# Moving query pieces and context splits inside an attention kernel's hand-written order, and issuing its weight and value loads from SyncE

## The chip, the cores and the metric

The kernel runs on one core of a Trainium2 chip, as one launch. The metric is the device time of that launch in microseconds, and the median of several runs is compared. TensorE is called PE in the profile, VectorE DVE, ScalarE ACT, GpSimd POOL and SyncE SP.

## What is computed

One attention block over 16 images of 30 by 30 tokens (900 tokens) with 512 channels and 8 heads of 64, all in f32:

```
q, k, v = x @ wq + bq, x @ wk + bk, x @ wv + bv          # per head, 64 channels
scores  = q @ k.T / sqrt(64) + spatial_bias[|dh| + |dw|]
ctx     = softmax(scores) @ v
resid   = ctx @ wo + bo + x
out     = layernorm(resid) * gamma + beta
```

## The kernel before

**Tiling.** Heads are taken in pairs, four pairs an image (`PAIRS`). A pair has 15 units (`PER_PAIR`), and a unit is two grid rows of queries against all 900 keys, for both heads. So an image has 60 units (`UNITS`). The kernel counts units within an image; unit 60 is unit 0 of the next image.

**The steps of a unit.** PE computes `scores` into one of two PSUM slots (L734). DVE adds the spatial bias and takes the smallest value (`biased_scores`, L1035). ACT takes the exponentials (`exponentials`, L862). POOL joins the halves of each softmax sum (`leads`, `totals`, L1174 to L1191), with one small exponential on ACT in between (`ratios`, L870). ACT multiplies by the weight (`normalise`, L878). DVE transposes (`turn`, L1052). After five units PE multiplies by the values (`context`, L752) and ACT keeps the result (`keep_context`, L893). There are three such groups in a pair and twelve in an image.

**Four engines, one written order.** Each engine runs a `body(im, u)` for every unit in order, and the engines meet only through semaphores. At step u PE issues the scores of units u+6 and u+7 (even u only, `AHEAD` is 6), then contexts due at u (`PV_UNITS`), then the background work of `GAPS[u]`. DVE at step u does `biased_scores(u + 6)` and then `turn(u)`. ACT does what `EVICT` puts at u, the exponentials of u+6 and the normalisation of u+2. Scores of unit n wait until DVE has read unit n-2 from PSUM (`scores_min`).

**Background work.** Everything else that PE does stands in `GAPS`, in one list for all images:

```
("piece", p, j)   # projection for pair p: j = 0, 1 the two key halves, j = 2, 3 the two query halves
("value", t)      # value projection of 128 tokens of the next image
("out", t)        # output projection of 128 tokens of the image before
```

Pieces of pair 4 and pair 5 are those of pairs 0 and 1 of the next image. Each of these jobs is 12 matmuls into one of two PSUM banks, which alternate in the order of the list (`BANK`). A job waits until the bank's last content was evicted. Pieces are evicted by ACT (`keep_piece`, L813), out tiles by DVE (`out_sum` from L1066, `out_norm` L1080), values by ACT (`stage_value`, L835). Pieces use weights in `w_sb`, one buffer for keys and one for queries, which is loaded anew for each pair (`next_weights`, L791). The values of a pair come from DRAM in four loads (`load_values`, L852, at the units of `LOADS`).

**Out tiles.** Before PE can do ("out", t), POOL splits the context tile into a high and a low part (`split_context`, L1202 and L1204, at the units of `SPLIT_UNITS`). It also adds the bias to the residual (`add_bias`, L1240) and makes the reciprocal deviation (`reciprocal_std`, L1246, L1249) that `out_norm` waits for. In the first image there are no out tiles.

**Queues.** SyncE issues all loads of x, the residuals, the stores of the output and of staged values, each behind the waits of its own order (`load_x` L538, `load_residual` L542, `store` L554, `keep_value` L524). ScalarE issues `next_weights` and `load_values` between its computations.

Of the kernel before, what the change touches and what calls it, by code (L numbers as in the profile page):

```python
# [17 lines left out]
NT = FULL + 1  # L18
# [18 lines left out]
KEY, QUERY = 0, 1  # L37
PIECES = [(KEY, 0), (KEY, 1), (QUERY, 0), (QUERY, 1)]
# [8 lines left out]
SPLIT_UNITS = [0, 0, 3, 5, 9, 13, 15]  # L47
# [23 lines left out]
def out(t):  # L71
    return ("out", t)


GAPS = {2: [out(0)] + pieces(1, (3,)), 4: [out(1)], 8: [out(2)] + pieces(2, (0,)), 12: [out(3)] + pieces(2, (1,)),
        14: [out(4)] + pieces(2, (2,)), 18: [out(5)] + pieces(2, (3,)), 22: [out(6)] + pieces(3, (0,)), 24: pieces(3, (2, 1)),
        28: pieces(3, (3,)), 32: [value(0), value(1)], 34: [value(2)], 38: [value(3), value(4)], 42: [value(5), value(6)],
        44: pieces(4, (0,)), 48: pieces(4, (1, 2)), 52: pieces(4, (3,)) + pieces(5, (0,)), 54: pieces(5, (1,)),
        58: pieces(5, (2,))}
# [8 lines left out]
PROLOGUE = [("first_xt", t) for t in range(NT)] + pieces(4) + [value(t) for t in range(NT)] + pieces(5, (0, 1, 2)) + [("bv_wo", 0)]  # L88
PROLOGUE_STEPS = {-6: [value(0), value(1), value(2)], -4: [value(3), value(4), value(5)],
                  -2: [value(6), value(7)] + pieces(5, (0, 1, 2)) + [("bv_wo", 0)]}  # L90
# [173 lines left out]
def attention_layernorm(nc, x, wq, bq, wk, bk, wv, bv, wo, bo, gamma, beta, spatial_bias, out):  # L264
# [3 lines left out]
    with ExitStack() as ctx:  # L268
# [202 lines left out]
        def _(sp):  # L471
# [59 lines left out]

            def load_x(b, t, a):

                n = x_rows(t)
                blocks, m = -(-n // QUAD), min(QUAD, n)
                part = bass.AP(tensor=x.tensor, offset=x.offset + (b * S + XB * t) * D + QUAD * a,
                               ap=[[D, m], [128, KT], [QUAD * D, blocks], [1, QUAD]])
                sp.dma_start(x_nat[QUAD * a:QUAD * a + m, x_slot(t), 0:KT * blocks * QUAD].rearrange(  # L538
                    "p (k b c) -> p k b c", k=KT, b=blocks), part).then_inc(x_in[x_slot(t)], 16)
# [16 lines left out]
            def body(im, u):  # L556
# [5 lines left out]
                if u < 0:  # L562
                    for work in PROLOGUE_STEPS.get(u - 1, []):
                        if work[0] == "value":
                            keep_value(pro, work[1])
                            if work[1] == FULL:
                                rest_values(0)
                    if u == -5:
                        for dst, src in ((bo_all, bo), (gamma_all, gamma), (beta_all, beta)):
                            sp.dma_start(dst[:, :], src.rearrange("(a d) -> a d", a=1).broadcast_to([TT, D])  # L570
                                         ).then_inc(small_in, 16)
                        keep_split(QUERY, "wq0", "wq", wq_split, wq_kept)
                    return
                for work in im.out_tiles(u - 4) + im.finals(u - 2):
                    store(im, work)
# [38 lines left out]
        def _(pe):  # L614
# [96 lines left out]
            def scores(im, u):  # L711
# [4 lines left out]
                if v == 0:  # L716
                    of = pro if im.first and u == 0 else im
                    for bank in range(BANKS):

                        mine = pieces(PAIRS if of is pro else p, (3,) if p == 1 else range(4))  # L720
                        mine = [of.use(use) + 1 for use in mine if bank_of(use) == bank]
                        if mine:
                            pe.wait_ge(bank_free[bank], max(mine))
                        elif p == 1:
                            pe.wait_ge(bank_free[bank], im.start(bank))
# [57 lines left out]
        def _(act):  # L783
# [20 lines left out]
            def keep_piece(im, p, j):  # L804
# [10 lines left out]
                if half and not (im is pro and p == PAIRS) and not (im.last and p == PAIRS - 1):  # L815
                    next_weights(kind, p)
# [21 lines left out]

            def load_values(im, p, n):

                b, p = (im.b, p) if p < PAIRS else (im.b + 1, 0)
                pair = PAIRS * b + p
                if n == 0:
                    if p == 0:
                        for i in range(STAGES):
                            act.wait_ge(v_kept[i], kept_in(i, b + 1))
                        act.wait_ge(v_rest_in, 16 * (b + 1))
                    if pair > 1:
                        act.wait_ge(pv_full, PAIR_GROUPS * (pair - 1))
                a, r = divmod(n, 2)  # L850
                row = 2 * QUAD * a + QUAD * r
                act.dma_start(values[row:row + QUAD, p % 2, :, :],  # L852
                              v_dram[b % 2, r, :, 128 * p:128 * p + 128].rearrange("(j k) d -> k j d", k=QUAD)
                              ).then_inc(v_in[p % 2], 16)
# [81 lines left out]
            def body(im, u):  # L936
# [29 lines left out]
                if im.first and u == 0:  # L966
                    use = ("bv_wo", 0)
                    act.wait_ge(bank_full[bank_of(use)], pro.use(use) + 1)
                    act.wait_ge(lo_done["wo"], 1)
                    for i in range(4):  # L970
                        load_values(im, 0, i)
                if u in LOADS and not (im.last and LOADS[u][0] == PAIRS):
                    load_values(im, *LOADS[u])
# [174 lines left out]
        def _(pool):  # L1148
# [103 lines left out]
            def body(im, u):  # L1252
# [21 lines left out]
                for t in range(FULL):  # L1274
                    if SPLIT_UNITS[t] == u and not im.first:
                        split_context(im, ("out", t))
                for t in range(NT):
# [39 lines left out]
```

## Time and profile before

| | |
|---|---|
| median of 3 runs | 3052.43 us (3050.78 to 3055.47) |
| the profiled execution's own time | 3046.97 us |
| its span in the trace | 3045.2 us |
| PE, DVE, ACT, POOL busy | 96%, 85%, 88%, 63% of the span |
| mean granted TensorE clock | 0.992 of full speed |
| DMA | 265 MB, mean 87 GB/s |

All sums in this document are made in the time of the one profiled execution. The 16 images repeat one pattern, so one image can stand for fourteen others; the first image and the end of the last are different. An engine's idle time counts only where the chain of work to the end passes through it.

### The profile page before, as it was taken

Reading aid. Unit: us, or ns where it says so; the run is one execution under the profiler, and the core shown is the slowest. Engines: PE = TensorE matmul, PEld = TensorE weight load, DVE = VectorE, ACT = ScalarE, POOL = GpSimd, SP = SyncE. Lnnn points to the kernel's source line nnn. Section 1 sums busy time; section 2 is a strip of 40 time slices with the busy share of each in tenths; the row PEclk is TensorE's granted clock in tenths of the full one; section 3 lists DMA queues with packets and bytes.
Section 4 is the critical chain, followed back from the end, with each engine's and each line's share of the span. In section 5 each row is a group of like instructions: output and inputs, shape, how many; then the busy total and the mean of one; then the engine's idle time right before and its main releaser. Section 6 shows DMA issues by size and latency. Waiting matters only on the chain.

```text
span 3045.2 us, 110658 instructions
## 1 busy us (share of the span) xinstructions
PE 2924.2 (96%) x44224; PEld 2038.4 (67%) x44224; DVE 2593.9 (85%) x5520; ACT 2690.0 (88%) x6825; POOL 1919.3 (63%) x5138
## 2 busy tenths in 40 slices
PE   8899999999999999999999999999999999999986
PEld 5566667766666666766667676666666666666654
DVE  3888889798898988989798897988989888897996
ACT  4998998989889898998989989898898989989894
POOL 1457657576665766657576575766657666575753
PEclk9999999999999999999999999999999999999998
DMA  7222413224232232423324133242322324132220
GB/s 225 71 79 78 115 57 101 84 80 104 67 94 84 84 98 76 99 69 97 85 73 115 60 98 87 77 104 66 97 80 84 98 76 103 65 99 83 77 68 27
DMA packets 431051, 265.00 MB, mean 87 GB/s; under 512 B 236949, under 2 KB 368021, under 8 KB 430413
## 3 DMA queue, kind: packets, MB, share of 16 engines
q1 hardware_dynamic: 283302, 126.03, 16.3%
q10 hardware_dynamic: 147232, 131.88, 14.0%
q8 instruction: 348, 5.70, 0.8%
q14 instruction: 169, 1.38, 0.2%
HBM read 194.40 MB, written 63.57 MB: 85 GB/s over the span
## 4 chain that ended last, share of the span: by engine, by line
PE 65%; ACT 15%; POOL 11%; DVE 5%; issue 4%; ACTq 1%; DMA 0%; DVEq 0%; POOLq 0%; SPq 0%
PE s_ps L734 17%; PE pv_ps L752 17%; PE r_ps L654 14%; PE r_ps L669 10%; ACT prob L862 7%; PE r_ps L695 7%; ACT prob L878 6%; POOL ctx_split L1204 3%; DVE prob L1035 2%; POOL other L1174 2%; DVE prob_t L1052 2%; POOL weight L1191 2%; POOL tokens L1240 1%; POOL ctx_split L1202 1%; POOL lead L1180 1%
## 5 line engine op out<-in xcount | busy, mean ns | idle before, releaser
L1035 DVE CUSTOM_DVE_ANT_0 prob<-s_ps,window 128x450 f32<-128x450 f32 x1920 | 1122.7, 622 | 347.4 <-PE s_ps L734 274.9
L862 ACT ACTIVATE prob<-prob,own 128x450 f32<-128x450 f32 x1920 | 1265.8, 663 | 143.5 <-DVE own L1035 130.9
L878 ACT ACTIVATE prob<-prob,weight 128x450 f32<-128x450 f32 x1920 | 1173.7, 661 | 67.4 <-POOL weight L1191 67.4
L1052 DVE STREAM_TRANSPOSE prob_t<-prob 128x960 f32<-128x960 f32 x960 | 1126.0, 1173 | 0.3 <-ACT prob L878 0.2
L734 PE MATMUL s_ps<-k_sb,q_sb 64*32 64x450 f32 x15360 | 850.1, 546 | 62.4 <-DVE own L1035 61.6
L752 PEld LDWEIGHTS pv_ps<-prob_t,values 64*64 64x64 f32 x23040 | 727.9, 133 | 142.0 <-DVE prob_t L1052 81.7
L752 PE MATMUL pv_ps<-prob_t,values 64*64 64x150 f32 x23040 | 781.4, 289 | 0.2
L654 PE MATMUL r_ps<-xt,w_sb 128*128 128x450 f32 x3072 | 678.1, 372 | 9.8 <-ACT prob_t L835 4.5
L654 PEld LDWEIGHTS r_ps<-xt,w_sb 128*128 128x128 f32 x3072 | 571.8, 189 | 146.8 <-issue 83.0
L1186 POOL TENSOR_TENSOR lead<-lead,other 128x4 f32<-128x4 f32 x480 | 118.7, 247 | 725.8 <-ACT lead L870 695.1
L1191 POOL TENSOR_TENSOR weight<-lead,minus_one 128x4 f32<-128x4 f32 x480 | 500.7, 1043 | 37.7
L734 PEld LDWEIGHTS s_ps<-k_sb,q_sb 64*32 64x32 f32 x15360 | 231.5, 106 | 431.0 <-issue 291.7
L1174 POOL COPY other<-own 32x8 f32<-32x8 f32 x1920 | 364.0, 190 | 152.1 <-ACT prob L862 5.3
L695 PE MATMUL r_ps<-wo_sb,ctx_split 128*128 128x512 f32 x1356 | 351.9, 409 | 32.1 <-POOL ctx_split L1204 16.3
L862 ACT ACTIVATION_READ_ACCUMULATOR prob<-prob,own 128x1 f32 x1920 | 365.4, 190 | 0.0
L695 PEld LDWEIGHTS r_ps<-wo_sb,ctx_split 128*128 128x128 f32 x1356 | 251.1, 192 | 166.6 <-issue 110.6
L669 PE MATMUL r_ps<-wv_sb,xt 128*128 128x512 f32 x1344 | 327.0, 398 | 0.0
L669 PEld LDWEIGHTS r_ps<-wv_sb,xt 128*128 128x128 f32 x1344 | 247.5, 188 | 98.8 <-issue 45.9
L1035 DVE DVE_READ_ACCUMULATOR2_ANT own<- 128x1 f32 x1920 | 158.4, 83 | 0.0
L893 ACT ACTIVATE ctx_sb<-pv_ps 128x300 f32<-128x300 f32 x192 | 79.2, 413 | 86.9 <-PE pv_ps L752 86.1
L1204 POOL TENSOR_TENSOR ctx_split<-ctx_sb,ctx_split 128x512 fp32r<-128x512 f32 x105 | 140.1, 1334 | 8.6
L1224 POOL TENSOR_TENSOR xt<-x_turned,xt 128x512 fp32r<-128x512 f32 x120 | 138.7, 1156 | 10.3
(74 smaller groups left out, 1497.8 us busy)
## 6 DMA issues: line engine op xcount, KB each, us to landing
w_sb<-w_split ACTq DMA_DIRECT2D x126, 512.0 KB, 3.7
values<-v_dram ACTq DMA_DIRECT2D x256, 240.0 KB, 3.1
tokens<-in_x SPq DMA_DIRECT2D x109, 256.0 KB, 4.0
tokens<-in_x SPq DMA_DIRECT2D x420, 64.0 KB, 2.9
out<-tokens SPq DMA_DIRECT2D x105, 256.0 KB, 2.1
v_dram<-stage SPq DMA_DIRECT2D x75, 256.0 KB, 2.1
v_dram<-ctx_sb SPq DMA_DIRECT2D x15, 256.0 KB, 2.5
v_dram<-ctx_sb SPq DMA_DIRECT2D x15, 132.0 KB
```

Of the source, the lines that this page charges most:

```text
L654: last = pe.matmul(r_ps[:, bank, 0:HALF], w_sb[:, kind, a, k, :], xt[:, c, k, columns(half)], start=(k == 0 and i == 0), stop=(k == KT - 1 ...
L669: last = pe.matmul(r_ps[0:n, bank, :], rest_xt[:, a, k, :] if t == FULL else xt[:, a, k, at:at + n], wv_sb[:, c, k, :], start=(k == 0 and ...
L695: last = pe.matmul(r_ps[0:rows(t), bank, :], ctx_split[:, t % 2, a, k, 0:rows(t)], wo_sb[:, c, k, :], start=(k == 0 and i == 0), stop=(k = ...
L734: last = pe.matmul(s_ps[row:row + QUAD, u % 2, head, 0:HALF], q_sb[d, p % 2, q0:q0 + QUAD], k_sb[d, p % 2, columns(r)], start=True, stop=T ...
L752: last = pe.matmul(pv_ps[d, a, 0:n * GRID].rearrange("d (u w) -> d u w", u=n), values[half, p % 2, j, d], prob_t[half, g % 2, 0:n, head, Q ...
L862: nc.scalar.activation(prob[:, im.unit(u) % RING, head, 0:HALF], prob[:, im.unit(u) % RING, head, 0:HALF], ACT.Exp, scale=-1.0, bias=own[: ...
L878: nc.scalar.activation(prob[:, im.unit(u) % RING, head, 0:HALF], prob[:, im.unit(u) % RING, head, 0:HALF], ACT.Copy, scale=weight[:, s, c: ...
L1035: nc.vector.tensor_tensor_reduce(prob[:, im.unit(u) % RING, head, 0:HALF], s_ps[:, u % 2, head, 0:HALF], window[:, w0:w0 + HALF // GRID, : ...
L1052: nc.vector.transpose(out=prob_t[:, g % 2, v % PER_GROUP, :, :].rearrange("p h k -> p (h k)"), in_=prob[:, im.unit(u) % RING, :, :].rearra ...
L1174: nc.gpsimd.tensor_copy(other[QUAD * a:QUAD * a + QUAD, s, :, :], own[QUAD * c:QUAD * c + QUAD, s, :, :]).then_inc(exchanged, 1)
L1191: nc.gpsimd.tensor_tensor(weight[:, s, :], total[:, s, :], minus_one[:, :], ALU.pow).then_inc(weight_done, 1)
L1204: nc.gpsimd.tensor_tensor(ctx_split[:, t % 2, 1, :, 0:m], src, ctx_split[:, t % 2, 0, :, 0:m].bitcast(F32), ALU.subtract).then_inc(split_l ...
```

## The change

Six edits:

1. `GAPS`: in the steady pattern one piece, ("piece", 5, 2), leaves unit 58 of the image before and becomes ("piece", 1, 2) at unit 2, and ("piece", 1, 3) moves from unit 2 to unit 4. The pieces (5, 0) and (5, 1) move from units 52 and 54 to 54 and 58. So unit 52 has one piece instead of two, and unit 4 has an out tile and a piece instead of an out tile alone.
2. `SPLIT_UNITS`: the splits of out tiles 0 and 1 move from unit 0 to units -3 and -1, which are units 57 and 59 of the image before.
3. `NEEDS`: the scores of a pair's first unit wait for both key halves and the first query half; the second query half is waited for only at the pair's unit 7, which is the first that reads it.
4. `EARLY`: the prologue computes pieces (5, 0) and (5, 1), no longer (5, 2).
5. `next_weights` is issued by SyncE at the unit of eviction, behind a wait for the piece's matmuls. (Three of these loads in the prologue stay on ScalarE.)
6. `load_values` is issued by SyncE at the same units as before, with the same waits.

```
+NEEDS = {0: (0, 1, 2), HALF // (2 * GRID): (3,)}
...
-SPLIT_UNITS = [0, 0, 3, 5, 9, 13, 15]
+SPLIT_UNITS = [-3, -1, 3, 5, 9, 13, 15]
...
-GAPS = {2: [out(0)] + pieces(1, (3,)), 4: [out(1)], 8: [out(2)] + pieces(2, (0,)), 12: [out(3)] + pieces(2, (1,)),
+GAPS = {2: [out(0)] + pieces(1, (2,)), 4: [out(1)] + pieces(1, (3,)), 8: [out(2)] + pieces(2, (0,)), 12: [out(3)] + pieces(2, (1,)),
...
-        44: pieces(4, (0,)), 48: pieces(4, (1, 2)), 52: pieces(4, (3,)) + pieces(5, (0,)), 54: pieces(5, (1,)),
-        58: pieces(5, (2,))}
+        44: pieces(4, (0,)), 48: pieces(4, (1, 2)), 52: pieces(4, (3,)), 54: pieces(5, (0,)), 58: pieces(5, (1,))}
...
+EARLY = [j for j in range(4) if ("piece", PAIRS + 1, j) in SEQUENCE]
+PROLOGUE = [("first_xt", t) for t in range(NT)] + pieces(4) + [value(t) for t in range(NT)] + pieces(5, EARLY) + [("bv_wo", 0)]
...
+            def next_weights(im, p, j):
+                kind, half = PIECES[j]
+                use = ("piece", p, j)
+                bank = bank_of(use)
+                sp.wait_ge(bank_full[bank], im.use(use) + 1)
+                sp.dma_start(w_sb[:, kind, :, :, :].bitcast(F32), w_split[(p + 1) % PAIRS, :, kind]
+                             ).then_inc(w_in[kind], 16)
...
+                for work in im.evicted(u):
+                    if work[0] == "piece" and PIECES[work[2]][1] and not (im.last and work[1] == PAIRS - 1):
+                        next_weights(im, *work[1:])
+                if im.first and u == 0:
+                    use = ("bv_wo", 0)
+                    sp.wait_ge(bank_full[bank_of(use)], pro.use(use) + 1)
+                    sp.wait_ge(lo_done["wo"], 1)
+                    for i in range(4):
+                        load_values(im, 0, i)
+                if u in LOADS and not (im.last and LOADS[u][0] == PAIRS):
+                    load_values(im, *LOADS[u])
...
-                if v == 0:
-                    of = pro if im.first and u == 0 else im
+                if v in NEEDS:
+                    of = im if p else pro if im.first else Image(im.b - 1, first=im.b == 1)
...
-                        mine = pieces(PAIRS if of is pro else p, (3,) if p == 1 else range(4))
+                        mine = pieces(p or PAIRS, [j for j in NEEDS[v] if p != 1 or j not in EARLY])
...
+                    if SPLIT_UNITS[t] == u - UNITS and not im.last:
+                        split_context(Image(im.b + 1), ("out", t))
```

## Rows read from the trace of the kernel before

**Rows 1.** Page: engines, busy us, share of the span, instructions.

```profile
PE 2924.2 (96%) x44224; PEld 2038.4 (67%) x44224; DVE 2593.9 (85%) x5520; ACT 2690.0 (88%) x6825; POOL 1919.3 (63%) x5138
```

**Rows 2.** Waits of the whole span: us in total, times, longest us.

```profile
PE s_ps L734 <- DVE own L1035: 61.6, 59, 1.7
...
PE r_ps L695 <- POOL ctx_split L1204: 16.3, 15, 1.1
```

**Rows 3.** PE waits of the last image, 2836 to 3045 us.

```profile
PE s_ps L734 <- DVE own L1035: 15.5, 15, 1.7
```

**Rows 4.** Timeline, PE, from an image's unit 52: start, us, work, idle before.

```profile
962.07 5.17 PE L654 MATMUL r_ps<-xt,w_sb 128*128 128x450 f32 x24
...
983.14 4.06 PE L752 MATMUL pv_ps<-prob_t,values 64*64 64x150 f32 x120
987.13 1.74 PE L734 MATMUL s_ps<-k_sb,q_sb 64*32 64x450 f32 x32
989.96 3.04 PE L695 MATMUL r_ps<-wo_sb,ctx_split 128*128 128x512 f32 x12 [1.09 <-POOL ctx_split L1204]
...
1006.65 0.99 PE L734 MATMUL s_ps<-k_sb,q_sb 64*32 64x450 f32 x16 [0.86 <-DVE own L1035]
1009.15 0.99 PE L734 MATMUL s_ps<-k_sb,q_sb 64*32 64x450 f32 x16 [1.52 <-DVE own L1035]
...
1022.89 0.99 PE L734 MATMUL s_ps<-k_sb,q_sb 64*32 64x450 f32 x16 [0.75 <-DVE own L1035]
```

**Rows 5.** Timeline, DVE, the same stretch.

```profile
978.25 0.63 DVE L1035 CUSTOM_DVE_ANT_0 prob<-s_ps,window 128x450 f32<-128x450 f32 x1 [0.46 <-PE s_ps L734]
...
981.76 1.18 DVE L1052 STREAM_TRANSPOSE prob_t<-prob 128x960 f32<-128x960 f32 x1
...
1004.50 1.01 DVE L1080 SCALAR_TENSOR_TENSOR tokens<-tokens,rstd,beta_all 128x512 f32<-128x512 f32 x1 [1.00 <-POOL rstd L1249]
1005.43 0.61 DVE L1035 CUSTOM_DVE_ANT_0 prob<-s_ps,window 128x450 f32<-128x450 f32 x1
```

**Rows 6.** Timeline, ACT and its queue, the same stretch.

```profile
960.54 0.42 ACT L893 ACTIVATE ctx_sb<-pv_ps 128x300 f32<-128x300 f32 x1 [1.06 <-PE pv_ps L752]
...
971.68 0.33 ACTq L791 DMA_DIRECT2D w_sb<-w_split  x1
971.81 0.61 ACT L813 ACTIVATE k_sb<-r_ps,bk_col 128x450 f32<-128x450 f32 x1
...
979.01 1.23 ACT L878 ACTIVATE prob<-prob,weight 128x450 f32<-128x450 f32 x2
...
994.60 1.23 ACT L878 ACTIVATE prob<-prob,weight 128x450 f32<-128x450 f32 x2 [2.31 <-POOL weight L1191]
```

**Rows 7.** Timeline, POOL, around the first two splits of an image.

```profile
984.68 0.20 POOL L1186 TENSOR_TENSOR lead<-lead,other 128x4 f32<-128x4 f32 x1 [2.27 <-ACT lead L870]
...
987.84 0.61 POOL L1202 CAST ctx_split<-ctx_sb 128x512 fp32r<-128x512 f32 x1
```

**Rows 8.** Lines L852 and L791: issue ns, min/median/max, then issue to landing.

```profile
L852 ACTq DMA_DIRECT2D values<-v_dram x256: 309/310/512, 77.2 to 2957.3; - x128
...
DMA to landing us min/median/max: 2.9/3.1/7.6
```

**Rows 9.** Timeline, DVE, transpose of x tile 6 of the next image.

```profile
1106.06 0.71 DVE L1023 STREAM_TRANSPOSE x_turned<-tokens 128x512 f32<-128x512 f32 x1 [0.53 <-DMA tokens<-in_x]
...
1110.60 0.63 DVE L1035 CUSTOM_DVE_ANT_0 prob<-s_ps,window 128x450 f32<-128x450 f32 x1 [1.66 <-PE s_ps L734]
```

**Rows 10.** Timeline, PE and DVE, end of the prologue and first image.

```profile
61.78 9.18 PE L654 MATMUL r_ps<-xt,w_sb 128*128 128x450 f32 x36 [4.49 <-ACT prob_t L835]
...
74.50 0.69 DVE L1130 TENSOR_TENSOR bo_all<-r_ps,bo_all 128x512 f32<-128x512 f32 x1 [17.42 <-PE r_ps L681]
...
86.60 0.99 PE L734 MATMUL s_ps<-k_sb,q_sb 64*32 64x450 f32 x16 [0.59 <-DVE own L1035]
89.01 1.54 PE L734 MATMUL s_ps<-k_sb,q_sb 64*32 64x450 f32 x16 [1.43 <-DVE own L1035]
```

## The prediction on record

> **What bounds the kernel now.** Four views, in this order. The page's first part shows PE busy 96% of the span and no other engine over 88% [rows 1], so PE is asked first what it waits for. The waits of the whole span give two kinds worth having in the steady images: scores that wait for DVE to read PSUM, 61.6 us, and out tiles that wait for POOL's split, 16.3 us in 15 waits, one for each image that has out tiles [rows 2]. The timeline of one image puts them in place: 1.09 us ahead of out tile 0 at unit 2, then 0.86 and 1.52 us at unit 8 and 0.75 us at unit 12, together 4.22 us [rows 4]. From unit 14 on to the next image's unit 2 PE has no idle row. The timelines of DVE, ACT and POOL say why, and what comes next.
>
> DVE's part: unit 4 gives PE only scores and an out tile, while DVE has out_sum of tile 0, out_sum of tile 1 and out_norm of tile 0 to add to its usual two units. It also stands 1.00 us in out_norm for POOL's rstd [rows 5]. So the scores of unit 14 are released by a DVE that starts unit 12 only at 1005.43. POOL's part: its splits start at 987.84, behind the softmax work of unit 0 [rows 7], and two of them, a bias add and a third split push everything after them back. ACT waits 2.31 us for a weight in the same place [rows 6].
>
> Does 4.22 us an image hold for all? Image 0 has no out tiles, so 15 images: 63.3 us. The totals agree: 61.6 less the last image's 15.5, less image 0's 4.2 (its four waits for DVE), plus the 3.1 of the last image's own units 8 to 12, is 45.0 us, and with 16.3 it is 61.3 [rows 2 to 4, 10].
>
> **The change part by part.** *Work.* No engine gets more or less of it. Each piece is 12 matmuls, 2.65 us of PE (two in a row took 5.17 [rows 4]; one alone adds its start). One piece an image goes from the stretch of units 52 to 58 to unit 4. In the balance of PE alone that is zero.
>
> *The splits at -3 and -1.* The split of tile 0 is ready about 10 us before PE wants it: it needs the context of unit 50, which ACT keeps at 960.54 [rows 6]. The wait of 1.09 goes whole: -16.3 us over 15 images. The new place costs POOL one split of 1.9 us (0.61 and 1.28, by L1202's row and its neighbour) after the `leads` of units 56 and 58. There POOL stands 2.27 us idle for ACT's ratio [rows 7]. So 0.4 us of cover is left, and `totals` is not late. If the cover were gone, ACT's normalisation would be late by the difference, and behind it `turn`.
>
> *The piece at unit 4.* I compare two times, both counted from the scores of unit 8 at 987.13, which unit 2 issues. PE's demand: it was free for the scores of unit 14 at 1006.65 - 0.86 = 1005.79, which is 18.7; without the 1.09 and with the piece this becomes 20.2. DVE's supply: it started on unit 12 at 1005.43, which is 18.3; without the 1.00 for rstd (POOL's queue then has neither the two splits nor what they held up) that is 17.3, and reading a unit takes 1.1, so 18.4. The wait of 0.86 is gone with 1.8 us over. The wait of 1.52 is for unit 13, which DVE reads 2.4 us later (20.8) while PE asks 0.9 later (21.1): gone with 0.3 us over, and this leaves out that DVE also idled between for PE's scores. The 0.75 at unit 12 is the same lag carried on, and goes with it. Together -3.13 us an image, -47 us over 15.
>
> *The gap that the piece leaves.* This is where something comes back. Units 52, 54 and 58 now give PE 4.3 us each (scores 1.67, a piece 2.65), and DVE needs 4.7 for two units (from 978.25 to the end of the transpose of 981.76) [rows 5]. PE would reach the scores at 987.13 2.65 us sooner. ACT has no idle row from 960.54 to 992 [rows 6], so it gets there sooner by only the eviction that left, 0.52 us (its row says 0.61; the next instruction starts 0.52 on). The last `turn` that PE's context at 983.14 needs ran from 981.76 [rows 4, 5], behind the normalisation of 979.01, which is done at about 980.1 [rows 6]. With ACT 0.52 sooner that is 979.6, and the transpose ends at about 980.8. PE wants it at 983.14 - 2.65 = 980.5. So PE waits some 0.3 to 0.5 us there, and I take 0.4: +6 us over 15 images. The bounds are 0 (PE's demand and DVE's supply just meet) and 1.9 (all of 2.65 less 0.52 and less the 0.2 between transpose and context before). I go near the low end because this normalisation was done 1.6 us before its transpose began, and that slack is there to be used.
>
> *`NEEDS`.* Before, ACT's eviction of piece (4, 3) was hidden from PE by piece (5, 0) behind it, and no row shows a wait at unit 54. With (5, 0) gone, the old wait would hold unit 54's scores until that eviction. The new waits ask for this half only at the pair's unit 7. So the edit keeps PE from a wait of at most the 2.65 us of cover lost, and brings nothing of its own: 0.
>
> *Loads on SyncE.* ACT's row of 0.33 us for an issue lies under its neighbour: the next computation starts at 971.81 with no idle before it [rows 6]. So the 24 issues an image cost ACT nothing now, and taking them off gives 0. A load takes about 3 us to land [rows 8]. Weights are used at least one background slot with a context after the piece that frees them, over 10 us; the values of a pair 8 units or more after their load. On SP the loads stand behind `store`, `keep_value` and `load_x`, and those behind them: `load_x` of tile 6 comes after a values load of unit 35. That tile's transpose already waits 0.53 us for its DMA, but two units later DVE idles 1.66 us for PE [rows 9]. One issue (0.31 us) is covered. Cost 0.
>
> The Trainium skill (*DMA: Bandwidth & Descriptors*, "Issuing engines are not separate DMA queues") says that issuing from several engines saves only the sequencer's time. The trace agrees for ACT only in that the issue has a duration. If each issue did cost ACT its 0.31 to 0.34 us, ACT would be 7.7 us an image freer, the 0.4 above would be 0, and the sum 6 us lower.
>
> *Prologue and image 0.* The prologue has three pieces in 9.18 us, then `bv_wo`, and DVE waits 17.42 us for that [rows 10]. One piece less is -3.06. At unit 4 image 0 gets a piece of 2.7 us, which takes the place of waits of 0.59 and 1.43 at unit 6 [rows 10], but both of its query pieces use one bank in image 0, and the second waits some 0.7 us for ACT's eviction. Net -1.7, bounds -3.1 and +1.
>
> **The sum.** -63.3 + 6 - 1.7 = -59, and with the totals of rows 2 in place of one image's rows -57. I take -58: 3046.97 becomes 2989. The profiled execution lies 5.5 us below the median of the runs shown, so the median goes from 3052.4 to about 2995 (-1.9%).
>
> **The rivals.** *A: ACT holds the end of each image.* PE gets only ACT's 0.52 us of the 2.65. For it: ACT without idle for over 30 us [rows 6]. Against it: 1 us and more of slack ahead of the transposes. Per image 4.22 - 1.9 = 2.3, in all 35 + 1.7: 3052 - 36 = 3016. Chance 0.14.
>
> *B: DVE still holds units 8 and 12.* The 0.3 us ahead of unit 13's reads is thin. If DVE comes 1.5 us late out of unit 2 (turns waiting for ACT), the wait returns. 4.22 - 0.4 - 1.5 = 2.3: also about 3016. Chance 0.11.
>
> *C: slower.* SP's order makes x tiles late. At units 35 and 37 two values loads go ahead of tiles 6 and 7. If the tile's transfer were to queue behind each in full, 3.1 us each [rows 8], DVE would be 6.2 us late, less 1.66 of cover: 4.5 us an image against 3.8 won. 14 images by 0.7 is +10: about 3062. It decides from a delay of 5.5 us on. Against it: today the same loads share the DMA engines with the tiles, and 0.53 us is all that a tile is late [rows 9]. Chance 0.04.
>
> The same page of the Trainium skill ("Queues, rings and completion order") says that what one engine issues is consumed in order in its rings. This is what C would rest on; no row here shows two such loads in one ring, and the page gives no time for it.
>
> *D: no change.* Each gain given back elsewhere to within 6 us. Chance 0.03.
>
> **The numbers.** Forecast 0.68, 2986 to 3004: from all waits gone and nothing back (66 us) to a loss of 1 us an image. A and B lie at 3016 and reach to 3022 with the ends of image 0. So 2985 to 3022 leaves 2 in 10 out at most. 0.2% (6 us) is about what a measurement of this kernel can tell from no change. Faster: forecast, A and B, 0.93. Same 0.03, slower 0.04.
>
> **What would show it.** Right: no wait of L695 for ctx_split; no wait of L734 for L1035 at units 8 and 12; each image shorter by about 3.8 us; PE over 97% busy. The step on the gap: waits of L752 for L1052, or of L734 for L1035, late in the image. C: waits of L1023 for tokens<-in_x of over 1 us. Wrong would be the forecast if ACT's idle time falls near zero (A), or if DVE's rows at unit 8 come as late as before (B).

## The result, and the profile after

The changed kernel takes 3004.78 us (median of 4 runs, 3001.49 to 3008.08), beside 3051.93 us for the kernel before in the same comparison (4 runs, 3050.78 to 3055.47). The ratio is 0.9848, with an interval of 0.9836 to 0.9861: 1.5% faster. Forecast were 2995 us and 1.9%. The forecast's own range ended at 3004 and rivals A and B stood at 3016, so the time lies just outside the one and inside the whole range of 2985 to 3022. The profiled execution took 3001.49 us, 45.5 less than the one profiled before.

In the page of the changed kernel, the engines' line, two lines of the DMA queues and the issues answer to [rows 1, 8] (columns of the issues: KB each, median us from issue to landing):

```profile
PE 2926.6 (98%) x44224; PEld 2038.2 (68%) x44224; DVE 2605.2 (87%) x5520; ACT 2688.8 (90%) x6825; POOL 1918.5 (64%) x5138
...
q1 hardware_dynamic: 427990, 253.46, 33.6%
q8 instruction: 348, 5.70, 0.8%
...
w_sb<-w_split SPq DMA_DIRECT2D x123, 512.0 KB, 4.7
values<-v_dram SPq DMA_DIRECT2D x256, 240.0 KB, 5.3
```

No engine's work changed by more than 0.5%; the span fell and PE's share rose from 96% to 98%. What did change is the loads: the values land after 5.3 us instead of 3.1, the weights after 4.7 where the page before has 3.7.

PE's waits over the steady stretch, 240 to 2795 us (us in total, times, longest):

```profile
PE s_ps L772 <- DVE own L1048: 8.3, 9, 1.0
PE pv_ps L790 <- issue: 2.7, 3, 1.1
PE s_ps L772 <- issue: 1.1, 4, 0.5
```

Lines have moved: L772 is the scores' L734, L1048 DVE's reading of them (L1035), L733 the out tile (L695). Before, the same stretch had 41.9 us in 40 waits for DVE and 15.2 us in 14 waits for POOL's split. The second kind is gone altogether. The first has shrunk to one wait in 9 images, 8 of them of 1.0 us. A new kind is there, of 3.8 us (3.6 of them within the 14 periods counted below): gaps that the profile puts down to "issue", so to nothing that it shows.

One image in the timelines, PE from unit 0 on, answers to [rows 4]:

```profile
424.56 4.06 PE L790 MATMUL pv_ps<-prob_t,values 64*64 64x150 f32 x120
428.55 1.74 PE L772 MATMUL s_ps<-k_sb,q_sb 64*32 64x450 f32 x32
430.22 3.06 PE L733 MATMUL r_ps<-wo_sb,ctx_split 128*128 128x512 f32 x12
...
437.31 3.07 PE L733 MATMUL r_ps<-wo_sb,ctx_split 128*128 128x512 f32 x12
440.22 2.63 PE L692 MATMUL r_ps<-xt,w_sb 128*128 128x450 f32 x12
...
450.43 1.17 PE L772 MATMUL s_ps<-k_sb,q_sb 64*32 64x450 f32 x16 [1.01 <-DVE own L1048]
451.54 3.07 PE L733 MATMUL r_ps<-wo_sb,ctx_split 128*128 128x512 f32 x12
```

The context at 424.56 starts without a wait, and so does the out tile at 430.22. Of the four waits of [rows 4] one is left, at unit 8. DVE in the same stretch answers to [rows 5]:

```profile
428.81 1.18 DVE L1065 STREAM_TRANSPOSE prob_t<-prob 128x960 f32<-128x960 f32 x1 [0.54 <-ACT prob L899]
...
434.06 1.18 DVE L1065 STREAM_TRANSPOSE prob_t<-prob 128x960 f32<-128x960 f32 x1 [0.32 <-ACT prob L899]
...
445.01 1.76 DVE L1093 SCALAR_TENSOR_TENSOR tokens<-tokens,rstd,beta_all 128x512 f32<-128x512 f32 x1
446.70 0.61 DVE L1048 CUSTOM_DVE_ANT_0 prob<-s_ps,window 128x450 f32<-128x450 f32 x1
```

and POOL beside the last two:

```profile
443.40 0.58 POOL L1262 TENSOR_TENSOR rstd<-var_eps,constants 128x1 f32<-128x1 f32 x1
...
444.63 1.60 POOL L1217 TENSOR_TENSOR ctx_split<-ctx_sb,ctx_split 128x512 fp32r<-128x512 f32 x1
```

`rstd` is now there in time: `out_norm` of tile 0 (L1093) begins without a wait. But it takes 1.76 us, and ends 0.5 us after POOL's split (L1217, tile 3). Before, it waited 1.00 us and took 1.01 [rows 5].

**Where 45.5 us came from.** Counted from the first out tile of one image to that of the next, 14 periods took 184.64 us each before and 181.61 after: -42.5 us. The start, up to the first out tile, is 2.3 us shorter (251.77 to 249.46), and the rest of the last image only 0.7. Over the 14 periods the waits for DVE and POOL fell from 57.1 to 8.3 us, by 48.8. So 6.3 us were lost again: 3.6 in the gaps put down to issue, 2.7 in rows of PE that got longer.

### The profile page after: what moved, and what is told of

It is laid out like the page before. It is cut to its first block, busy times and chain, and to the rows that moved or that the text cites. A ratio compares the mean times of both kernels' runs of the same rounds, so it can differ in the third digit from the quotient of the medians.

```text
span 2999.7 us, 110722 instructions
## 1 busy us (share of the span) xinstructions
PE 2926.6 (98%) x44224; PEld 2038.2 (68%) x44224; DVE 2605.2 (87%) x5520; ACT 2688.8 (90%) x6825; POOL 1918.5 (64%) x5138
## 4 chain that ended last, share of the span: by engine, by line
PE 79%; ACT 13%; DVE 5%; issue 2%; POOL 0%; DMA 0%; SPq 0%; DVEq 0%; ACTq 0%; POOLq 0%
PE s_ps L772 21%; PE pv_ps L790 21%; PE r_ps L692 17%; PE r_ps L707 11%; PE r_ps L733 9%; ACT prob L883 6%; ACT prob L899 5%; DVE prob L1048 1%; DVE prob_t L1065 1%; DVE tokens L1093 1%; DVE stats L1081 1%; ACT ctx_sb L914 0%; DVE tokens L1079 0%; ACT k_sb L851 0%; ACT lead L891 0%
## 5 line engine op out<-in xcount | busy, mean ns | idle before, releaser
L1048 DVE CUSTOM_DVE_ANT_0 prob<-s_ps,window 128x450 f32<-128x450 f32 x1920 | 1122.9, 622 | 305.6 <-PE s_ps L772 227.4
L899 ACT ACTIVATE prob<-prob,weight 128x450 f32<-128x450 f32 x1920 | 1174.3, 662 | 12.8 <-POOL weight L1204 12.8
L1065 DVE STREAM_TRANSPOSE prob_t<-prob 128x960 f32<-128x960 f32 x960 | 1126.2, 1173 | 14.3 <-ACT prob L899 12.1
L772 PE MATMUL s_ps<-k_sb,q_sb 64*32 64x450 f32 x15360 | 853.8, 546 | 25.9 <-DVE own L1048 23.9
L1204 POOL TENSOR_TENSOR weight<-lead,minus_one 128x4 f32<-128x4 f32 x480 | 507.0, 1056 | 37.7
L772 PEld LDWEIGHTS s_ps<-k_sb,q_sb 64*32 64x32 f32 x15360 | 233.1, 106 | 395.8 <-issue 307.6
L1187 POOL COPY other<-own 32x8 f32<-32x8 f32 x1920 | 353.4, 184 | 151.7 <-ACT prob L883 5.0
L733 PE MATMUL r_ps<-wo_sb,ctx_split 128*128 128x512 f32 x1356 | 349.8, 408 | 16.2 <-DVE ctx_split L1100 14.6
L733 PEld LDWEIGHTS r_ps<-wo_sb,ctx_split 128*128 128x128 f32 x1356 | 249.3, 190 | 148.6 <-issue 93.0
L1048 DVE DVE_READ_ACCUMULATOR2_ANT own<- 128x1 f32 x1920 | 157.9, 82 | 0.0
L1217 POOL TENSOR_TENSOR ctx_split<-ctx_sb,ctx_split 128x512 fp32r<-128x512 f32 x105 | 140.5, 1338 | 8.7
```

The source lines that it names most:

```text
L733: last = pe.matmul(r_ps[0:rows(t), bank, :], ctx_split[:, t % 2, a, k, 0:rows(t)], wo_sb[:, c, k, :], start=(k == 0 and i == 0), stop=(k = ...
L772: last = pe.matmul(s_ps[row:row + QUAD, u % 2, head, 0:HALF], q_sb[d, p % 2, q0:q0 + QUAD], k_sb[d, p % 2, columns(r)], start=True, stop=T ...
L899: nc.scalar.activation(prob[:, im.unit(u) % RING, head, 0:HALF], prob[:, im.unit(u) % RING, head, 0:HALF], ACT.Copy, scale=weight[:, s, c: ...
L1048: nc.vector.tensor_tensor_reduce(prob[:, im.unit(u) % RING, head, 0:HALF], s_ps[:, u % 2, head, 0:HALF], window[:, w0:w0 + HALF // GRID, : ...
L1065: nc.vector.transpose(out=prob_t[:, g % 2, v % PER_GROUP, :, :].rearrange("p h k -> p (h k)"), in_=prob[:, im.unit(u) % RING, :, :].rearra ...
L1187: nc.gpsimd.tensor_copy(other[QUAD * a:QUAD * a + QUAD, s, :, :], own[QUAD * c:QUAD * c + QUAD, s, :, :]).then_inc(exchanged, 1)
```

## The experiments

Each period below is the mean over the same 14 images of one profiled execution. The ratios are against the kernel before, measured on the same chip.

### The order alone, and the loads alone

```
# order alone: the changed kernel, but next_weights and load_values issued by ScalarE
-                sp.dma_start(w_sb[:, kind, :, :, :].bitcast(F32), ...
-                sp.dma_start(values[row:row + QUAD, p % 2, :, :], ...
+                act.dma_start(w_sb[:, kind, :, :, :].bitcast(F32), ...
+                act.dma_start(values[row:row + QUAD, p % 2, :, :], ...
...
# loads alone: the changed kernel with GAPS, SPLIT_UNITS, NEEDS and EARLY as before; its loads stay on SyncE
```

> The new order of pieces and splits, with the loads of weights and values issued by ScalarE as before. Theory 1 (the gain is the order's; an issue costs ScalarE nothing): 3000 us, within 6 us of the changed kernel's 3004.8. The wait of scores at unit 8 stays at about 1.0 us in most images. If the short PE gaps put down to issue in the changed kernel (1 to 2.5 us in four of 14 images) come from loads that SyncE issues in bursts, they are gone, and the time is 4 us below the changed kernel. Theory 2 (freeing ScalarE of 24 issues an image brings a good part of the gain): over 3015 us, and ScalarE's normalisation is later ahead of the transposes.

> The order of before, with only the loads of weights and values moved to SyncE. Theory 1: 3052 us, up to 5 us more if load bursts stretch PE's gaps. Theory 2: 3040 us or less.

The order alone: 3001.94 us, ratio 0.984 (0.9825 to 0.9855), period 181.53. The loads alone: 3053.08 us, 1.0007 (0.9998 to 1.0017), period 184.81. So the whole gain is the order's, and issuing from SyncE brings nothing and costs nothing that these runs can tell. In the order alone 13 of 15 images have the wait of 0.9 to 1.0 us at unit 8, and gaps put down to issue are there as well, fewer and smaller (1.7 us in 3 over the whole span, one of 0.81 us just ahead of an image's out tile 0, beside 4.5 us in 8 in the changed kernel). So SyncE's issuing is not the only thing that makes the gaps. In the loads alone such gaps occur too, but a wait stands behind them: after one of 0.51 us the wait for the split is 0.18 instead of 1.09 us. The period there is only 0.17 us above that of the kernel before.

### The pieces alone, and the splits alone

```
# pieces alone: GAPS, NEEDS, EARLY as in the change, loads on ScalarE, and
-SPLIT_UNITS = [-3, -1, 3, 5, 9, 13, 15]
+SPLIT_UNITS = [0, 0, 3, 5, 9, 13, 15]
# splits alone: the kernel before with
-SPLIT_UNITS = [0, 0, 3, 5, 9, 13, 15]
+SPLIT_UNITS = [-3, -1, 3, 5, 9, 13, 15]
...
+                    if SPLIT_UNITS[t] == u - UNITS and not im.last:
+                        split_context(Image(im.b + 1), ("out", t))
```

> The new places of the pieces (with the waits by half), but the splits of out tiles 0 and 1 at unit 0 as before, loads on ScalarE. Theory 1 (the splits have to move for the pieces' move to pay): GpSimd's split of tile 0 comes only some 0.5 us sooner while PE comes 2.6 us sooner, so the wait ahead of out tile 0 grows from 1.1 to about 3.2 us; per image about 1 us is won and the time is 3035 us. Rival (the parts add up independently): the wait stays 1.1 us and the time is that of the changed kernel plus 16 us, 3021 us.

> Only the splits of out tiles 0 and 1 moved to units -3 and -1, all else as before. Theory 1: the wait of 1.09 us ahead of out tile 0 goes, VectorE's wait for rstd gets shorter too, and 1.1 to 2 us an image is won: 3022 to 3036 us. Rival (what is won at unit 2 is waited for at unit 8, since VectorE sets the pace there): 3050 us, with the waits at unit 8 grown from 2.4 to 3.5 us.

The pieces alone: 3046.43 us, 0.9987 (0.9978 to 0.9996), period 184.53. The splits alone: 3016.62 us, 0.9887 (0.9872 to 0.9902), period 182.45. PE's rows with waits, first of two images of the pieces alone, then of one image of the splits alone:

```profile
437.41 4.54 PE L696 MATMUL r_ps<-wo_sb,ctx_split 128*128 128x512 f32 x12 [2.73 <-POOL ctx_split L1205]
...
622.91 3.04 PE L696 MATMUL r_ps<-wo_sb,ctx_split 128*128 128x512 f32 x12 [2.72 <-POOL ctx_split L1205]
```

```profile
452.86 0.99 PE L734 MATMUL s_ps<-k_sb,q_sb 64*32 64x450 f32 x16 [0.40 <-DVE own L1035]
...
455.37 0.99 PE L734 MATMUL s_ps<-k_sb,q_sb 64*32 64x450 f32 x16 [1.52 <-DVE own L1035]
```

Without the splits, the moved pieces only bring PE 2.6 us sooner to out tile 0, whose split isn't there: the waits at unit 8 are traded for one of 2.73 us, and in eight images 0.7 us stay at unit 12. In the other seven the wait is followed by something else: PE's granted clock falls to the lower of its two levels (1.2 GHz instead of 2.4), and out tile 0 takes 4.3 to 4.6 us instead of 3.04. The mean granted clock (column PEclk, the third from the end) is 0.66 over the first of the two out tiles above and 1.00 over the second:

```profile
437.00:442.00 5.00, 4.59 (x14) 3.71 (x15) 2.32 (x6) 2.73 (x10) 4.72 (x7) 0.66 0.02 3
622.00:627.00 5.00, 4.09 (x18) 3.50 (x19) 3.58 (x8) 3.24 (x10) 4.76 (x7) 1.00 0.01 5
```

The same wait stands ahead of both, so it doesn't by itself decide whether the clock falls. Most images without such a stretch and without a gap take 183.94 to 184.00 us, some 0.5 less than the most frequent period before (184.52). Neither theory fits the time of the pieces alone: the wait grew as the first one said, but even that one expected 3035 us. Among the other kernels, the one before has two such stretches in its steady images (periods of 185.12 and 185.03), the loads alone two and the splits alone three (183.55 to 183.97 where most take about 182.0). The changed kernel has none.

The splits alone gained more than either theory said. They remove more than their own wait: the 1.09 goes, the 0.86 shrinks to 0.40, the 0.75 at unit 12 goes too, and only the 1.52 stays. DVE reaches unit 8 earlier because POOL has two splits fewer in front of `rstd`. I had given that effect to the piece at unit 4.

### What holds unit 8: POOL's split of tile 3

```
-SPLIT_UNITS = [-3, -1, 3, 5, 9, 13, 15]
+SPLIT_UNITS = [-3, -1, 3, 8, 9, 13, 15]
```

> The changed kernel with the split of out tile 3 at unit 8 instead of 5. In the changed kernel GpSimd's split (1.60 us) lies beside VectorE's last step of out tile 0 (1.76 us instead of 0.71). Theory 1 (this step waits for GpSimd's instruction to end, and the 1.05 us is the whole of the wait of 1.0 us that is left at unit 8): the step takes 0.7 to 0.8 us, the wait at unit 8 goes in nearly all images, and the time is 2990 us, 10 to 15 below the changed kernel. Rival (another GpSimd instruction takes the split's place, or the delay comes from elsewhere): 3003 to 3006 us with the wait still at 1.0 us.

2996.41 us (2994.61 to 2999.16), ratio 0.9824 (0.981 to 0.9839), beside 0.9848 (0.9836 to 0.9861) for the changed kernel. So the time lies between the two theories, and the rows decide. DVE's `out_norm` of tile 0 and POOL in the same place:

```profile
442.53 0.75 DVE L1085 SCALAR_TENSOR_TENSOR tokens<-tokens,mean_var,gamma_all 128x512 f32<-128x512 f32 x1
443.20 0.75 DVE L1093 SCALAR_TENSOR_TENSOR tokens<-tokens,rstd,beta_all 128x512 f32<-128x512 f32 x1
```

```profile
442.67 0.67 POOL L1199 TENSOR_TENSOR lead<-lead,other 128x4 f32<-128x4 f32 x1 [0.29 <-ACT lead L891]
443.42 0.58 POOL L1202 TENSOR_TENSOR lead<-lead,own 128x4 f32<-128x4 f32 x1
444.08 1.01 POOL L1204 TENSOR_TENSOR weight<-lead,minus_one 128x4 f32<-128x4 f32 x1
```

With the split out of the way the last step of `out_norm` takes 0.75 us instead of 1.76, and in none of the 15 images has PE a wait for DVE at unit 8. Now POOL's small operations stretch, from 0.20 to 0.67 and 0.58 us, while DVE's two run. The Trainium skill (*SBUF — State Buffer*, "Who interferes with whom") says that a DVE instruction with two inputs in SBUF contends with a GpSimd instruction that reads SBUF, that the shared ports are an exclusive lock, and that the order of issue decides which of the two waits. Both traces agree: whichever of the two comes second ends late (1.76 for 0.75 on DVE, 0.67 for 0.20 on POOL). The trace of the kernel before had shown it already. There the last step of `out_norm` for tile 1 starts just behind POOL's `add_bias` (1010.58) and takes 1.71 us, where it takes 0.71 in most of its rows:

```profile
1010.72 1.71 DVE L1080 SCALAR_TENSOR_TENSOR tokens<-tokens,rstd,beta_all 128x512 f32<-128x512 f32 x1 [0.62 <-POOL rstd L1249]
```

The period of the kernel with the later split is 181.37 all the same, since gaps put down to issue took more: 7.4 us in the whole span.

### What also feeds unit 8: ACT late in the image

```
-                nc.scalar.activation(dst[:, p % 2, columns(half)], r_ps[:, bank, 0:HALF], ACT.Identity,
+                n = 8 if p > PAIRS and im is not pro else HALF
+                nc.scalar.activation(dst[:, p % 2, half * HALF:half * HALF + n], r_ps[:, bank, 0:n], ACT.Identity,
```

This leaves out 442 of the 450 columns of the eviction of pieces (5, 0) and (5, 1).

> The changed kernel, but ScalarE evicts only 8 of 450 columns of the two pieces of the next image's second pair at units 54 and 58 (this leaves out part of the keys). ScalarE gets about 0.8 us freer late in the image. Theory 1 (ScalarE's lag there is the other half of VectorE's delay, 0.54 and 0.32 us of transposes that wait for it): those waits shrink to under 0.2 us together, the wait at unit 8 falls from 1.0 to about 0.2 us, and the time is 2993 us. Rival (that lag is caught up before unit 8): the wait stays 1.0 us and the time 3004 us.

2995.08 us (2992.34 to 2996.92), ratio 0.9817 (0.9801 to 0.9834), period 181.07. DVE waits only 1.9 us for the normalisation (12.1 us in 27 waits in the change), and the wait at unit 8 is down to a third:

```profile
448.40 1.38 PE L772 MATMUL s_ps<-k_sb,q_sb 64*32 64x450 f32 x16 [0.33 <-DVE own L1049]
```

So the 1.01 us at unit 8 has at least two sources, DVE's late transposes (0.54 and 0.32 us) and the long last step of `out_norm` (1.0 us too long). Together they are more than PE's wait, and so taking away the first leaves 0.33 and taking away the second leaves nothing. Two smaller ones of the second kind lie in the same stretch of the image shown above: the step of `out_norm` before the last (L1085) takes 1.20 us for tile 0, beside POOL's `add_bias`, and 0.93 for tile 1, beside the first part of the split, instead of 0.75. No run takes them away by themselves.

### The second split somewhere else

```
-SPLIT_UNITS = [-3, -1, 3, 5, 9, 13, 15]
+SPLIT_UNITS = [-3, -3, 3, 5, 9, 13, 15]
```

> The changed kernel with both first splits at unit -3. Theory 1 (GpSimd's 2.3 us of idle time there hide one split of 1.9 us and no more): the second split makes the softmax weights 1.5 us late, ScalarE waits for them, the transposes after it, and the wait at unit 8 grows by up to 1 us: 3010 to 3020 us. Rival (the slack of the chain takes it): 3005 us.

3021.31 us, ratio 0.9907 (0.9892 to 0.9922), period 182.91: the first theory, and 1 us more than its range. DVE's waits and ACT's, whole span:

```profile
DVE prob_t L1065 <- ACT prob L899: 29.4, 45, 1.1
```

```profile
ACT prob L899 <- POOL weight L1204: 28.4, 32, 1.1
```

In the change these are 12.1 us in 27 waits and 12.8 us in 18. Two splits in one place need 3.8 us of POOL's time where about 2.3 stood idle [rows 7]; the rest goes through `totals`, the weight, the normalisation and the transpose into a wait of 1.52 us at unit 8.

### The old rule for the first scores of a pair

```
-                if v in NEEDS:
-                    of = im if p else pro if im.first else Image(im.b - 1, first=im.b == 1)
+                if v == 0:
+                    of = pro if im.first and u == 0 else im
...
-                        mine = pieces(p or PAIRS, [j for j in NEEDS[v] if p != 1 or j not in EARLY])
+                        mine = pieces(PAIRS if of is pro else p, (2, 3) if p == 1 else range(4))
...
```

> The changed kernel with the old rule for the scores of a pair's first unit: they wait for all pieces of the pair. Theory 1 (piece (4,3) has lost the piece behind it that hid its eviction): PE waits at unit 54 for ScalarE, 1 to 2.6 us an image, of which some is slack that VectorE and ScalarE need anyway; 3010 to 3040 us. Rival (ScalarE is on time, the new rule is idle): 3005 us.

3013.77 us (3013.59 to 3013.92), ratio 0.988 (0.9866 to 0.9895). PE at unit 54:

```profile
406.06 2.73 PE L692 MATMUL r_ps<-xt,w_sb 128*128 128x450 f32 x12
410.51 1.75 PE L772 MATMUL s_ps<-k_sb,q_sb 64*32 64x450 f32 x32 [1.72 <-issue]
```

ACT's eviction of that piece starts at 409.80 in this trace and its next instruction at 410.31: the scores start just behind it. The profile names no releaser here, so that the wait is for this eviction is read from the two times and from the edit. `NEEDS` is worth 9 us, less than 1.72 an image. One reason can be seen: the wait at unit 8 is gone in this kernel, probably since PE asks for its scores later.

### What the gaps put down to issue are

```
# with split 3 at unit 8, SyncE issuing
-                sp.dma_start(w_sb[:, kind, :, :, :].bitcast(F32), w_split[(p + 1) % PAIRS, :, kind]
+                sp.dma_start(w_sb[:, kind, :, 0:1, :].bitcast(F32), w_split[(p + 1) % PAIRS, :, kind, :, 0:1]
...
-                sp.dma_start(values[row:row + QUAD, p % 2, :, :],
+                m = BLOCKS if im.first else 3
+                sp.dma_start(values[row:row + QUAD, p % 2, 0:m, :],
...
```

This leaves out three quarters of each weight load, and four fifths of the values after the first image. All engines' instructions stay.

> The kernel with the split of tile 3 at unit 8, with each weight load cut to 128 of 512 KB and each value load of later images to 3 of 15 blocks (this leaves out three quarters of the next weights and four fifths of the values). With all waits gone in that kernel, its images still differ: 180.4 to 183.1 us, by PE gaps put down to issue. Theory 1 (these are PE's instruction fetches, late behind the bursts of the loads): images of 180.3 to 180.6 us throughout, gaps gone, 2983 to 2987 us. Rival (they do not come from this traffic): 2994 to 2998 us, gaps as before.

2982.35 us (2978.17 to 2984.11), ratio 0.9769 (0.9756 to 0.9782). The 14 periods lie between 180.35 and 180.40 us, and PE has no wait at all in them. That is what one image of before gives without its waits (184.52 - 4.22 = 180.30). So the gaps come with the load traffic. In the changed kernel, the DMA view of 2240 to 2250 us (40 slices of 0.25 us) beside PE's rows there:

```profile
GB/s 82 164 311 344 197 197 221 277 330 315 229 133 74 72 53 57 18 8 10 16 20 0 0 0 0 0 66 0 10 96 137 297 313 96 14 18 0 0 0 0
```

```profile
2240.65 3.79 PE L790 MATMUL pv_ps<-prob_t,values 64*64 64x150 f32 x111
2245.59 0.59 PE L790 MATMUL pv_ps<-prob_t,values 64*64 64x150 f32 x9 [1.15 <-issue]
```

The gap falls in the middle of a context, between two matmuls that wait for nothing new, and follows two bursts of over 300 GB/s. A third one in the same 10 us (313 GB/s at 2248) is followed by none.

The page lists a DMA queue of kind instruction with 5.70 MB in 348 packets. Divided by 2 x 44224, PE's matmuls and weight loads, that is 64 bytes each, and one packet of 16,384 bytes holds 256 of them. The traces bear this out. Number PE's matmuls and weight loads in the order of their starts. After the first 60 us, eleven of the traces have 56 gaps put down to issue (leaving out those of 1.7 us under the old rule), and all 56 stand at number 193 or 194 of a block of 256. The kernels before and with the small loads have none there. It is even the same matmul that stops in one kernel after the other, here the ninth from the end of that context in the kernel with split 3 at unit 8:

```profile
2240.34 0.59 PE L790 MATMUL pv_ps<-prob_t,values 64*64 64x150 f32 x9 [1.50 <-issue]
```

So the gaps are PE waiting for the next block of its own program. The waits of 1.7 us at unit 54 are of another kind: they stand at number 96, 24, 208 and so on of a block. How the loads make a block late is not shown: the last packets of this queue ahead of the gaps took 1.0 to 1.5 us in the changed kernel, beside a median of 1.1 for all in the steady images.

The changed kernel and the one with the small loads have the same 44224 matmuls in the same order, so the two traces can be laid side by side, start to start. Over the 14 periods the changed kernel is 17 us longer, 10.0 us of it at its waits for DVE and 6.7 at the ends of blocks. The page shows 8.3 and 3.6 for these. So most of the 2.7 us of longer rows are these same waits and pauses.

### The best combination

```
-SPLIT_UNITS = [-3, -1, 3, 5, 9, 13, 15]
+SPLIT_UNITS = [-3, -1, 3, 8, 9, 13, 15]
# and next_weights and load_values stay on ScalarE
```

> The kernel with the split of tile 3 at unit 8, and the loads issued by ScalarE. Theory 1 (with PE never waiting there is nothing left in which the loads' issuer could matter but the gaps, and spread issues stretch a fetch less): 2993 us, 0 to 6 below the kernel with SyncE's loads. Rival (with no slack left, ScalarE's 24 issues an image count): 3000 us or more.

2990.79 us (2987.43 to 2993.59), ratio 0.9797 (0.9783 to 0.981), period 180.63. It beats both kernels. Waits of PE for issue in the whole span are 0.8 us:

```profile
PE s_ps L735 <- issue: 0.4, 2, 0.2
PE pv_ps L753 <- issue: 0.2, 1, 0.2
PE r_ps L696 <- issue: 0.2, 1, 0.2
```

and its loads land sooner:

```profile
w_sb<-w_split ACTq DMA_DIRECT2D x126, 512.0 KB, 4.0
values<-v_dram ACTq DMA_DIRECT2D x256, 240.0 KB, 3.3
```

With SyncE issuing the ratio was 0.9824 (0.981 to 0.9839). The intervals just touch, so the times alone hardly tell the two apart, but the traces point the same way: 0.8 us of gaps against 7.4. A likely reason, not tested by itself: ACT issues each load between two computations, which spreads them, and SyncE as fast as its waits allow. This can't be told in the kernel before and in the changed one, where PE also has waits at unit 8 that can take up a pause (3001.94 and 3004.78 us for the changed order).

### Splits without any piece moved

```
# the kernel before with
-SPLIT_UNITS = [0, 0, 3, 5, 9, 13, 15]
+SPLIT_UNITS = [-3, -1, 3, 8, 9, 13, 15]
...
+                    if SPLIT_UNITS[t] == u - UNITS and not im.last:
+                        split_context(Image(im.b + 1), ("out", t))
```

> Only the splits moved (tiles 0 and 1 to units -3 and -1, tile 3 to unit 8), pieces and loads as in the kernel before. Theory 1 (what held PE at unit 8 was mostly GpSimd's splits beside VectorE's norm steps, not the missing piece at unit 4): of the 1.93 us an image left with the two splits moved, 1.05 goes, and the time is 3002 us, as good as the whole change. Rival (the piece at unit 4 is needed for the rest): 3012 to 3016 us.

3005.01 us (3002.41 to 3006.93), ratio 0.9845 (0.9831 to 0.9858), period 181.57. Each image has one wait left:

```profile
450.92 0.99 PE L734 MATMUL s_ps<-k_sb,q_sb 64*32 64x450 f32 x16 [1.29 <-DVE own L1035]
```

Three numbers in one line, and the two lines of code that let a split stand in the image before, give as much as the whole change. With the pieces moved as well and the same splits the kernel takes 2991 with the same issuer of the loads.

## Why the prediction was right, and where it was not

**Right.** PE is what bounds, and its waits for DVE and POOL are what there was to win: 48.8 of 57.1 us went. The split's wait of 1.09 us went whole, under the cover that was worked out for one split (0.4 us; POOL still idles 0.33 us there), and with two splits in that place the cover is gone, as costed. The loads on SyncE bring 0. `NEEDS` protects against a wait of up to 2.65 us (1.72 seen). Rival A didn't come: PE got 48.8 of the 57.1 us, and ACT still idles in 10% of the span. Rivals C and D didn't come either: over the whole span DVE's transposes of x tiles wait 1.2 us for their DMA.

**Wrong by 11.5 us in the trace** (57 by the totals, 45.5 measured). It splits like this:

*"The 1.00 us for rstd" (+2.7).* The step said that without this wait DVE begins unit 8's reads 1.00 us sooner. But a wait of 1.00 and an operation of 1.01 became one operation of 1.76: only 0.25 came of it. The "0.3 us over" for unit 13's reads was thereby spent. Then the transposes came 0.54 and 0.32 us late, and 1.01 us came back at unit 8 in most images, 8.3 us in all. I had looked at when POOL has `rstd` ready, and not at what POOL does next while DVE uses it, though the 1.01 for an operation that takes 0.71 in most rows was a sign, and tile 1's 1.71 a plain one. This is rival B in a smaller size. Its cause, turns that wait for ACT, is one of the two sources (0.86 us instead of 1.5), and the other is not in it.

*"The gap that the piece leaves" (its +5.6 over 14 images is inside the 8.3).* The mechanism was right, the place was not. ACT's normalisation is late, by about what was worked out (0.3 to 0.5 us; the transpose waits 0.54). But PE's context doesn't wait for it. DVE carries the delay to unit 8, where it adds to the other. The two don't add up to two waits: the long `out_norm` without the late transposes costs PE 0.33 us, the late transposes without it nothing.

*Gaps with the load traffic (+6.3).* No term of the prediction. The kernel before shows none in its steady images (its mean period of 184.64 lies above the most frequent 184.52 mainly by the two stretches at the lower clock). With the loads on SyncE and the old order there are three, and they cost little, since a wait stood behind each. When PE has no waits left, each shows in full. The 6.3 is 3.6 of shown gaps and 2.7 of longer rows, part of which belongs to the waits of the first step.

*The last image (+2.0).* I counted it like the others. There the piece that unit 4 gains isn't saved at units 52 to 58, since no image follows: of 3.13 us of waits 2.65 go back to work. 2.7 less was forecast for the stretch, 0.7 came.

*Prologue and image 0 (+0.5).* Forecast -1.7 beside the 1.09, came -1.2. The second query piece of image 0 waits 1.79 us for ACT's eviction, where some 0.7 were forecast, and no row stood behind that 0.7.

**The attribution was wrong too, and no number of the result shows it.** The prediction gave 3.13 us an image to the piece at unit 4 and 1.09 to the splits. Alone, the splits bring 2.2 us an image and the pieces 0.1 (2.5 and 0.5 in images without a stretch at the lower clock or a gap). In my working the effect of POOL's shorter queue on `rstd` stood under the piece. The two edits open one bottleneck after the other, and whoever made only the one that looked larger would have gained 5 us of 47.

## What to carry to other kernels

Before counting a removed wait as a gain, read what the awaited engine does next: an operation that starts earlier may now overlap one that it contends with, and end hardly sooner (1.00 + 1.01 us became 1.76). Credit a chain of waits edit by edit, each tested alone, since the edit that frees the queue in front can carry most of it. And as the bounding engine gets near 100% busy, small gaps that its waits would have absorbed (0.2 to 1.5 us, with the traffic of the loads) become the next term; loads that are smaller or spread out are then worth trying.

## What the hardware showed that was not expected

- DVE's `scalar_tensor_tensor` on 128x512 with two SBUF inputs takes 0.71 us in most rows of `out_norm` and 1.76 us beside POOL's split. The split's second part takes 1.29 in most rows and 1.60 beside it.
- PE pauses of 0.2 to 1.6 us inside a run of matmuls occur with the loads, always at the same place of a block of 256 of its instructions (16,384 bytes, one packet of the queue of kind instruction), and are gone when the loads are cut to a quarter and less. Against the kernel with the small loads (180.38) a period is 0.25 us longer with ScalarE issuing (180.63) and 1.0 with SyncE (181.37).
- In the pieces alone the granted clock fell to the lower level behind a wait of PE (2.7 us, once 1.8) in seven images of fifteen, and not in the other eight (2.7 us, once 1.6). It made an out tile 1.3 to 1.5 us longer.
- 24 issues an image of 0.31 us each on ScalarE's queue cost its computations nothing that can be measured: 3001.94 with them, 3004.78 without.
